# Top-4 routing in an adaLN transformer block: all experts for all tokens, or 128-row tiles of the tokens that chose an expert

## The chip, the cores and the metric

One core of a Trainium2 chip runs the whole program in one launch. The metric is the device time of that core in microseconds, the median over runs. The core has TensorE (PE, matmuls into PSUM), VectorE (DVE), ScalarE (ACT), GpSimd (POOL), SyncE (SP, which only issues DMAs here) and 16 DMA engines that all queues share.

## What is computed

Two batches of 512 tokens, 256 channels. Each half of the block normalises the rows, scales and shifts them by values made from a condition vector, and adds a gated branch. The first branch is a gated linear recurrence with an MLP behind it. The second, which the change is about, is a mixture of experts:

```python
h = layernorm(x) * (1 + cb) + sb                       # (2, 512, 256)
scores = softmax(h @ gate_weight.T)                    # 16 experts
topk_weight, topk_idx = top_k(scores, 4)
for e in range(16):                                    # hidden width 176 each
    w_e = sum(where(topk_idx == e, topk_weight, 0))
    y = y + w_e[:, None] * glu_ffn(h, gate_up[e], down[e])
y = y + glu_ffn(h, shared_gate_up, shared_down)        # hidden width 352
x = x + gb * y
# glu_ffn(x, gu, d): g, u = split(x @ gu.T); (silu(g) * u) @ d.T
```

So of 1024 x 16 (token, expert) pairs, 4096 have a weight other than zero.

## The kernel before

Each engine runs its own list of steps, written out by hand in `TENSOR_PLAN`, `SCALAR_PLAN`, `VECTOR_PLAN` and `POOL_PLAN` (lines 79 to 118); a step name is a function and its arguments (`up.0.3` is `ff_up(0, 3)`), and semaphores join the lists. In the plans, work of batch 1 is woven into that of batch 0, one stage apart. An engine executes in its list's order, so a wait holds everything behind it on that engine.

Products of full precision are made of three fp32r matmuls: each operand is split into a high part, rounded to fp32r, and a low rest, and high x high, low x high and high x low are summed in PSUM. ScalarE writes the high parts, VectorE (activations) and GpSimd (weights, `low`, line 372) the rests. Other matmuls are plain fp32. Activations stand with channels on the partitions, 512 tokens of one batch in the columns.

In the second half, the MLP of the first branch ends with `down.b.7`; `tm` turns its sum to token rows, VectorE adds and gates it (`sum3`, `gated3`, `plus_x`, lines 985 to 999), takes statistics (`var3`), GpSimd takes the power -0.5 (`rstd`, line 430), `hn3` normalises, `t3` transposes back to channels, ScalarE applies scale and shift (`h3`, line 484), `logits` multiplies by the gate weights, and `lgsub`, `exp`, `topk` make the weights of the four chosen experts, zero for the others. `weights_out` transposes them, SP writes them to DRAM and reads each expert's row back broadcast over partitions (`load_gate`, line 330).

The 16 x 176 routed and 352 shared hidden units are laid end to end and cut into 25 slices of 128, of which 22 (`NR`) are routed. For each slice SP loads 384 KB of weights (`wmoe`), ScalarE and GpSimd split them, and for each batch `moe_up` makes 12 matmuls of 512 columns (lines 1399 to 1401), ScalarE applies silu (line 700), VectorE multiplies by the gate (line 1056) and by the up half (line 1060), both split the product (lines 706 and 1065), and `moe_down` adds 6 matmuls (lines 1432 to 1436) into two banks that sum over all 25 slices. Batch 1 follows batch 0 eight slices behind (`LEAD`), so the first slices of batch 0 stand in the plans between the last steps of batch 1's own gate, and from then on TensorE alternates between the batches. At the end `sum_out` scales by `gb`, `sum_to_tokens` (line 1454) transposes, `finish` (line 1092) adds and SP stores 256 KB pieces of `hm`.

Early in the plans, SP brings six chunks of 512 KB of the MLP's weights through two `stage` buffers (line 319), each after the chunk two before was split by GpSimd (lines 372, 416).

Of the kernel before, what the change touches and what calls it, by code (L numbers as in the profile page):

```python
# [5 lines left out]
FP32R = mybir.dt.float32r  # L6
ALU = mybir.AluOpType
# [37 lines left out]
GATES = 3
ORDER = [NR, NR + 1, *range(6), NR + 2, *range(6, NR)]


def tile_of(q):

    return ORDER[q % NM]


def step_of(b, i):

    return i + LEAD * b


def gated_tile(b, i):

    return tile_of(step_of(b, i)) < NR


def gate_number(b, i):

    return sum(gated_tile(b, j) for j in range(i))


def gate_pieces(t):

    edges = sorted({t * P, (t + 1) * P, *(e * FE for e in range(NE + 1) if t * P < e * FE < (t + 1) * P)})
    return [(a // FE, a - t * P, b - t * P) for a, b in zip(edges, edges[1:])]

# [6 lines left out]
    down.0.4 t2.1 up.0.7 down.0.5 up.1.0 down.0.6 down.0.7 up.1.1 tm.0 up.1.2 down.1.0 up.1.3 down.1.1 down.1.2 up.1.4  # L83
    t3.0 up.1.5 down.1.3 up.1.6 logits.0 down.1.4 down.1.5 up.1.7 wt.0 down.1.6 down.1.7 eup.0.0 tm.1 eup.0.1 eup.0.2
    edown.0.0 edown.0.1 eup.0.3 edown.0.2 eup.0.4 t3.1 eup.0.5 edown.0.3 eup.0.6 logits.1 edown.0.4 eup.0.7 edown.0.5
    edown.0.6 wt.1
# [4 lines left out]
    wsm.3 wsm.4 q.0 xconv.0 sqk.0 sqv.0 ig.0 rk.0 rv.0 ga.0 wsm.5 h1hi.1.0 h1hi.1.1 h1.1.0 h1.1.1 sqm.0 og.0 rm.0 q.1  # L91
    sqo.0 k.1 wsm.6 ro.0 v.1 gated.0 xconv.1 wo.0 ig.1 ga.1 rk.1 h2hi.0.0 h2hi.0.1 h2.0.0 h2.0.1 rv.1 silu.0.0 og.1
    hid.0.0 silu.0.1 sqm.1 hid.0.1 silu.0.2 rm.1 silu.0.3 sqo.1 ro.1 gated.1 hid.0.2 silu.0.4 wo.1 hid.0.3 hid.0.4
    silu.0.5 silu.0.6 hid.0.5 hid.0.6 h2hi.1.0 h2hi.1.1 silu.0.7 h2.1.0 h2.1.1 silu.1.0 hid.0.7 hid.1.0 acc.0 silu.1.1
    silu.1.2 hid.1.1 ehigh.0.0 silu.1.3 hid.1.2 silu.1.4 hid.1.3 h3.0 silu.1.5 silu.1.6 hid.1.4 hid.1.5 exp.0 hid.1.6
    ehigh.0.1 silu.1.7 ehigh.0.2 hid.1.7 acc.1 ehigh.0.3 esilu.0.0 ehid.0.0 esilu.0.1 ehid.0.1 esilu.0.2 ehid.0.2
    ehigh.0.4 esilu.0.3 ehid.0.3 ehigh.0.5 esilu.0.4 ehigh.0.6 h3.1 esilu.0.5 esilu.0.6 ehid.0.4 ehigh.0.7 ehid.0.5
    exp.1 ehid.0.6 esilu.0.7 ehigh.0.8 ehid.0.7 ehigh.0.9
# [10 lines left out]
    hidlo.1.5 topk.0 hidlo.1.6 prod.1.7 wt.0 hidlo.1.7 egated.0.0 sum3.1 egated.0.1 gated3.1 elo.0.0 egated.0.2 elo.0.1  # L109
    plus_x.1 var3.1 elo.0.2 egated.0.3 hn3.1 elo.0.3 egated.0.4 egated.0.5 elo.0.4 egated.0.6 lgsub.1 h3lo.1 elo.0.5  # L110
    elo.0.6 topk.1 egated.0.7 wt.1 elo.0.7
# [5 lines left out]
    rstd.0.3 elow.1 elow.2 elow.3 elow.4 rstd.1.3 elow.5 elow.6 elow.7  # L117
# [10 lines left out]
def adaln_block_kernel(nc, x, cT, wmod, par, wsm, wff, wout, wgate, wmoe, sel, mats, out):  # L128
    ctx = ExitStack()
    with ctx:  # L130
# [36 lines left out]
        gm = [sb(f"gm{b}", [P, KC, T]) for b in range(NB)]  # L167
# [49 lines left out]
        def s(name):  # L217
            return S[name]
# [64 lines left out]
        def _(sp):  # L283
# [1248 lines left out]
```

## Time and profile before

| | us |
|---|---|
| median of 3 runs | 386.26 |
| lowest, highest | 385.79, 460.69 |
| profiled execution, span from the first to the last instruction | 383.2 |
| TensorE busy in it | 368.9 (96%) |
| VectorE, ScalarE, GpSimd busy | 245.5, 200.2, 111.0 |
| DMA, mean over the span | 91 GB/s |

The profile is of one execution. Its page gives the span alone and no time around it; the lowest run, 385.79, is 2.6 us above the span. Matmuls are pipelined, and a matmul's busy time in the groups holds its way through the array; how often one can start is read from the distance of two.

### The profile page before, as it was taken

Reading aid. Unit: us, or ns where it says so; the run is one execution under the profiler, and the core shown is the slowest. Engines: PE = TensorE matmul, PEld = TensorE weight load, DVE = VectorE, ACT = ScalarE, POOL = GpSimd, SP = SyncE. Lnnn points to the kernel's source line nnn. Section 1 sums busy time; section 2 is a strip of 40 time slices with the busy share of each in tenths; the row PEclk is TensorE's granted clock in tenths of the full one; section 3 lists DMA queues with packets and bytes.
Section 4 is the critical chain, followed back from the end, with each engine's and each line's share of the span. In section 5 each row is a group of like instructions: output and inputs, shape, how many; then the busy total and the mean of one; then the engine's idle time right before and its main releaser. Section 6 shows DMA issues by size and latency. Waiting matters only on the chain.

```text
span 383.2 us, 4573 instructions
## 1 busy us (share of the span) xinstructions
PE 368.9 (96%) x1590; PEld 286.2 (75%) x1590; DVE 245.5 (64%) x439; ACT 200.2 (52%) x314; POOL 111.0 (29%) x94
## 2 busy tenths in 40 slices
PE   6997988999999999999999999999999999999995
PEld 3774656656788888888878888888888888888883
DVE  4799985796765484749593555655555565555664
ACT  3679968788745326544654443333343333344441
POOL 1492769400010030315433123211112311133310
PEclk9899999999999999999999999999999999999998
DMA  6911131000030010162524622344333333125321
GB/s 222 362 31 42 50 109 62 2 0 0 9 131 2 0 41 3 44 164 71 137 85 152 193 97 96 97 126 134 126 98 96 96 102 129 45 70 149 125 85 55
DMA packets 18967, 34.81 MB, mean 91 GB/s; under 512 B 2528, under 2 KB 6496, under 8 KB 18944
## 3 DMA queue, kind: packets, MB, share of 16 engines
q1 hardware_dynamic: 18944, 34.52, 28.8%
q8 instruction: 13, 0.21, 0.2%
q14 instruction: 10, 0.08, 0.1%
HBM read 33.39 MB, written 1.11 MB: 90 GB/s over the span
## 4 chain that ended last, share of the span: by engine, by line
PE 83%; DVE 7%; ACT 4%; DMA 2%; SPq 2%; issue 1%; POOL 0%; DVEq 0%; ACTq 0%
PE ps L1399 12%; PE ps L1401 12%; PE ps L1400 12%; PE ps L1432 6%; PE ps L1436 6%; PE ps L1433 6%; PE ps L1351 4%; PE ps L1356 4%; PE ps L1352 4%; PE ps L1117 3%; PE ps L1134 3%; PE ps L1118 3%; DMA w<-in_wsm 2%; DVE w L857 1%; PE ps L1303 1%
## 5 line engine op out<-in xcount | busy, mean ns | idle before, releaser
L372 POOL TENSOR_TENSOR wsm_lo<-w,wsm_hi 128x768 fp32r<-128x768 f32 (+1 forms) x40 | 71.2, 1784 | 204.1 <-ACT wsm_hi L694 183.2
L1399 PE MATMUL ps<-b_hi,wsm_hi 128*128 128x512 f32 x200 | 79.3, 396 | 0.0
L1401 PE MATMUL ps<-b_lo,wsm_hi 128*128 128x512 f32 x200 | 78.9, 395 | 0.0
L1400 PE MATMUL ps<-b_hi,wsm_lo 128*128 128x512 f32 x200 | 78.9, 395 | 0.0
L706 ACT ACTIVATE a_hi<-w 128x512 fp32r<-128x512 f32 x50 | 31.6, 632 | 86.4 <-DVE w L1060 83.5
L1056 DVE TENSOR_TENSOR w<-w,gate_b 128x512 f32<-128x512 f32 x44 | 43.1, 980 | 41.6 <-ACT w L700 41.6
L1065 DVE TENSOR_TENSOR a_lo<-w,a_hi 128x512 fp32r<-128x512 f32 x50 | 34.6, 693 | 31.6 <-ACT a_hi L706 31.5
L700 ACT ACTIVATE w<-ps 128x512 f32<-128x512 f32 x50 | 29.9, 597 | 34.7 <-PE ps L1401 34.6
L1399 PEld LDWEIGHTS ps<-b_hi,wsm_hi 128*128 128x128 f32 x200 | 37.7, 188 | 8.9 <-POOL wsm_lo L372 0.2
L1401 PEld LDWEIGHTS ps<-b_lo,wsm_hi 128*128 128x128 f32 x200 | 37.7, 188 | 8.9
L1400 PEld LDWEIGHTS ps<-b_hi,wsm_lo 128*128 128x128 f32 x200 | 37.7, 188 | 8.5
L1060 DVE TENSOR_TENSOR w<-w,ps 128x512 f32<-128x512 f32 x50 | 34.4, 688 | 14.9 <-PE ps L1401 11.4
L1432 PE MATMUL ps<-a_hi,wsm_hi 128*128 128x512 f32 x96 | 38.0, 396 | 0.0
L1433 PE MATMUL ps<-a_hi,wsm_lo 128*128 128x512 f32 x96 | 37.8, 394 | 0.0
L1436 PE MATMUL ps<-a_lo,wsm_hi 128*128 128x512 f32 x96 | 30.1, 394 | 0.0
L694 ACT ACTIVATE wsm_hi<-w 128x768 fp32r<-128x768 f32 x33 | 27.5, 834 | 0.1
L1351 PE MATMUL ps<-b_hi,wff_hi 128*128 128x512 f32 x64 | 26.7, 418 | 0.0
L1352 PE MATMUL ps<-b_hi,wff_lo 128*128 128x512 f32 x64 | 25.2, 394 | 0.0
L464 ACT ACT_TABLE_LOAD x17 | 21.8, 1283 | 1.0 <-PEq L1526 0.7
L1432 PEld LDWEIGHTS ps<-a_hi,wsm_hi 128*128 128x128 f32 x96 | 18.1, 188 | 4.2
L1436 PEld LDWEIGHTS ps<-a_lo,wsm_hi 128*128 128x128 f32 x96 | 18.1, 188 | 4.2
L1433 PEld LDWEIGHTS ps<-a_hi,wsm_lo 128*128 128x128 f32 x96 | 18.1, 188 | 4.2
(189 smaller groups left out, 581.7 us busy)
## 6 DMA issues: line engine op xcount, KB each, us to landing
w<-in_wmoe SPq DMA_DIRECT2D x33, 384.0 KB, 3.2
gate_b<-w_rows SPq DMA_DIRECT2D x16, 256.0 KB, 4.2
stage<-in_wff SPq DMA_DIRECT2D x4, 512.0 KB, 6.5
gate_b<-w_rows SPq DMA_DIRECT2D x8, 224.0 KB, 3.4
w<-in_wsm SPq DMA_DIRECT2D x3, 512.0 KB, 9.1
w<-in_x SPq DMA_DIRECT2D x3, 512.0 KB, 3.6
gate_b<-w_rows SPq DMA_DIRECT2D x8, 192.0 KB, 3.5
gate_b<-w_rows SPq DMA_DIRECT2D x8, 160.0 KB, 3.3
```

Source lines behind the costliest of these rows:

```text
L372: return nc.gpsimd.tensor_tensor(lo, raw, f32(hi), ALU.subtract)
L1056: nc.vector.tensor_tensor(first[:, j, :], W[b][1][:, j, :], gate_b[b][:, n % GATES, :], ALU.mult).then_inc(s(f"mprod{b}"), 1)
L1060: nc.vector.tensor_tensor(W[b][3][:, j, :], first[:, j, :], up_bank, ALU.mult).then_inc(s(f"mgated{b}"), 1)
L1065: nc.vector.tensor_tensor(a_lo[b][:, j, :], W[b][3][:, j, :], f32(a_hi[b][:, j, :]), ALU.subtract).then_inc(s(f"mlo{b}"), 1)
L1351: mm(out, wff_hi[:, k, o:o + P], b_hi[b][:, k, :], start=k == 0, stop=False)
L1352: mm(out, wff_lo[:, k, o:o + P], b_hi[b][:, k, :], start=False, stop=False)
L1399: mm(bank, mgu(wsm_hi, slot, k, which), b_hi[b][:, k, :], start=k == 0, stop=False)
L1400: mm(bank, mgu(wsm_lo, slot, k, which), b_hi[b][:, k, :], start=False, stop=False)
L1401: last = mm(bank, mgu(wsm_hi, slot, k, which), b_lo[b][:, k, :], start=False, stop=k == KC - 1)
L1432: mm(PS[2 * b][:, m, :], mdn(wsm_hi, slot, m), a_hi[b][:, j, :], start=i == 0, stop=False)
L1433: mm(PS[2 * b][:, m, :], mdn(wsm_lo, slot, m), a_hi[b][:, j, :], start=False, stop=False)
L1436: last = mm(PS[2 * b][:, m, :], mdn(wsm_hi, slot, m), a_lo[b][:, j, :], start=False, stop=False)
```

## The change

Only the pairs that exist are computed, in plain fp32. Its parts:

- `rank.b` (TensorE and VectorE) gives each pair the slot `1 + 1024 e + (number of earlier tokens that chose e)` by matmuls of the chosen-matrix with a triangle of ones. GpSimd scatters each token's row of 288 floats (256 channels, 16 weights, its number, padding) to its four slots in a DRAM array `xs_rows`, by 16 indirect DMAs of 128 rows per batch. ScalarE's `fill` has written an empty row, with a weight of zero and a spare number, to every one of the 16,512 slots before, and zeros to four arrays `acc_rows`.
- `rows.b`: TensorE, ScalarE and GpSimd make the modulated rows with tokens on the partitions.
- `table` makes, on every partition, for each of 47 tiles its first slot, its expert's offset into the up weights and into the down weights. 47 is the most that 4096 pairs in 16 groups can fill; tiles past the last one read empty rows.
- Weights of all experts are loaded once, unsplit: `wdown` over buffers that the first half used, `wup` over the MLP's weights when the MLP is done.
- The three shared slices are computed as before, for all tokens, now in the plans, and summed to `hm`.
- A loop over 47 tiles follows on every engine, with four stages one step apart (`xt`, `up`, `hid`, `down`). SP reads the slot from SBUF into a register and loads 128 rows (ring of four). TensorE transposes them, reads the offset, makes 2 matmuls of 352 columns, transposes the hidden 128x176 in two, reads the other offset, makes 2 matmuls of 256 columns. ScalarE copies `xT`, applies silu, copies `y` scaled with the row's weight. VectorE makes number and weight from the row, multiplies silu and up, copies `hT`. GpSimd adds `y` to one of the four `acc_rows` by an indirect, accumulating DMA.
- Then SP loads the four sums (2 x 512 KB each), VectorE adds them, multiplies by `gb` and adds to `hm`, and SP stores.

The plans, cut to where they differ:

```diff
 TENSOR_PLAN
-    ... tm.0 up.1.2 ... up.1.7 wt.0 down.1.6 down.1.7 eup.0.0 tm.1 eup.0.1 eup.0.2
-    edown.0.0 edown.0.1 eup.0.3 edown.0.2 eup.0.4 t3.1 eup.0.5 edown.0.3 eup.0.6 logits.1 edown.0.4 eup.0.7 edown.0.5
-    edown.0.6 wt.1
+    ... tm.0 rows.0 up.1.2 ... up.1.7 rank.0 down.1.6 down.1.7 eup.0.0 tm.1 rows.1
+    eup.0.1 edown.0.0 eup.0.2 t3.1 edown.0.1 logits.1 edown.0.2 eup.1.0 rank.1 eup.1.1 st.0 edown.1.0 eup.1.2 edown.1.1
+    edown.1.2 st.1
 SCALAR_PLAN
-    wsm.3 wsm.4 q.0 xconv.0 ...
+    wsm.3 wsm.4 q.0 fill xconv.0 ...
 VECTOR_PLAN
+    hidlo.1.5 topk.0 hidlo.1.6 prod.1.7 rank.0 hidlo.1.7 egated.0.0 sum3.1 gated3.1 elo.0.0 plus_x.1 var3.1 egated.0.1
+    hn3.1 elo.0.1 egated.0.2 h3lo.1 lgsub.1 elo.0.2 topk.1 egated.1.0 rank.1 table sum.0 elo.1.0 egated.1.1 finish.0
+    elo.1.1 egated.1.2 elo.1.2 sum.1 finish.1
 POOL_PLAN
-    rstd.0.3 elow.1 elow.2 elow.3 elow.4 rstd.1.3 elow.5 elow.6 elow.7
+    rstd.0.3 rows.0 elow.1 scatter.0.0 elow.2 scatter.0.1 rstd.1.3 scatter.0.2 rows.1 scatter.0.3 scatter.1.0
+    scatter.1.1 scatter.1.2 scatter.1.3
```

The new functions, cut:

```diff
+RW = C + 2 * NE
+NTILE = (NB * T * TOPK + NE * (P - 1)) // P
+XROWS = 1 + DUMMY + P
+AROWS = CAP + P
 # SP
+            sp.wait_ge(s("down_done"), NB * NF)
+            for k in range(KC):
+                for which in range(2):
+                    o = (2 * k + which) * P
+                    sp.dma_start(wup[:, k, which, :].rearrange("p (t n) -> p t n", n=P),
+                                 wmoe[0:NR, :, o:o + P].rearrange("t p n -> p t n")).then_inc(s("wexp_in"), 16)
+            sp.wait_ge(s("scattered"), 16 * NB * NT * TOPK)
+            sp.wait_ge(s("tab_ready"), 1)
+            for i in range(NTILE):
+                if i >= RING:
+                    sp.wait_ge(s("xt_psum"), i - RING + 1)
+                    sp.wait_ge(s("wv_ready"), i - RING + 1)
+                row = nc.sync.value_load(tab[0:1, 0, i:i + 1], min_val=1, max_val=1 + DUMMY)
+                sp.dma_start(xt[:, i % RING, :], xs_rows[bass.ds(row, P), :]).then_inc(xt_in[i % RING], 16)
 # GpSimd
+            def scatter(b, j):
+                if j == 0:
+                    pool.wait_ge(s("filled"), 16 * (1 + NACC))
+                    ...
+                    pool.wait_ge(s("slots_ready"), b + 1)
+                for k in range(TOPK):
+                    nc.gpsimd.indirect_dma_start(
+                        xs_rows[:, :], bass.IndirectOffsetOnAxis(slots[b][:, j, k:k + 1], 0), h3x[b][:, j, :], None
+                    ).then_inc(s("scattered"), 16)
+            def add_rows(i):
+                n = i % NACC
+                pool.wait_ge(s("y_sb"), i + 1)
+                pool.wait_ge(s("wv_ready"), i + 1)
+                if i >= NACC:
+                    pool.wait_ge(added[n], 16 * (i // NACC))
+                nc.gpsimd.indirect_dma_start(acc_rows[n][:, :], bass.IndirectOffsetOnAxis(ids[:, i:i + 1], 0),
+                                             ysb[n], None, compute_op=ALU.add).then_inc(added[n], 16)
 # ScalarE
+            def fill():
+                act.wait_ge(s("fill_ready"), 1)
+                act.dma_start(xs_rows[1:XROWS, :].rearrange("(r p) c -> p r c", p=P),
+                              empty.unsqueeze(1).broadcast_to([P, XROWS // P, RW])).then_inc(s("filled"), 16)
+                for n in range(NACC):
+                    act.dma_start(acc_rows[n][:, :].rearrange("(r p) c -> p r c", p=P),
+                                  empty[:, 0:C].unsqueeze(1).broadcast_to([P, AROWS // P, C])).then_inc(s("filled"), 16)
 # TensorE
+            def tile_up(i):
+                ...
+                pe.wait_ge(s("xt_sb"), i + 1)
+                if i >= 2:
+                    pe.wait_ge(s("h_ready"), i - 1)
+                e = nc.tensor.value_load(tab[0:1, 1, i:i + 1], min_val=0, max_val=(NE - 1) * FE)
+                for k in range(KC):
+                    last = mm(bank(1, i)[:, 0:2 * FE].rearrange("p (w n) -> p w n", w=2), xT[i % 2][:, k * P:(k + 1) * P],
+                              up[:, k, :, bass.ds(e, FE)], start=k == 0, stop=k == KC - 1)
+                last.then_inc(s("up_psum"), 1)
+            def tile_down(i):
+                ...
+                e = nc.tensor.value_load(tab[0:1, 2, i:i + 1], min_val=0, max_val=(NE - 1) * 2 * C)
+                for h in range(2):
+                    last = mm(bank(3, i)[:, 0:C], hT[i % 2][:, h * P:(h + 1) * P], down[:, bass.ds(e + h * C, C)],
+                              start=h == 0, stop=h == 1)
+                last.then_inc(s("y_psum"), 1)
+            for step in range(NTILE + 3):
+                if step < NTILE:
+                    xt_in_channels(step)
+                if 0 <= step - 1 < NTILE:
+                    tile_up(step - 1)
+                if 0 <= step - 2 < NTILE:
+                    hid_in_channels(step - 2)
+                if 0 <= step - 3 < NTILE:
+                    tile_down(step - 3)
```

## Rows read from the trace of the kernel before

**Rows 1.** The page: busy share of TensorE and its granted clock in 40 slices, tenths.

```profile
PE   6997988999999999999999999999999999999995
...
PEclk9899999999999999999999999999999999999998
```

**Rows 2.** The page: the chain that ended last, shares of the span by engine, by line.

```profile
PE 83%; DVE 7%; ACT 4%; DMA 2%; SPq 2%; issue 1%; POOL 0%; DVEq 0%; ACTq 0%
PE ps L1399 12%; PE ps L1401 12%; PE ps L1400 12%; PE ps L1432 6%; PE ps L1436 6%; PE ps L1433 6%; PE ps L1351 4%; PE ps L1356 4%; PE ps L1352 4%; PE ps L1117 3%; PE ps L1134 3%; PE ps L1118 3%; DMA w<-in_wsm 2%; DVE w L857 1%; PE ps L1303 1%
```

**Rows 3.** Busy us of each engine in a stretch of the expert stage.

```profile
206.00:340.00 134.00, 134.00 (x579) 108.65 (x578) 74.02 (x96) 51.14 (x80) 29.87 (x17) 1.00 0.36 111
```

**Rows 4.** The chain in order of time: start us, us, what.

```profile
40.06 1.72 PE ps L1303 x4
...
162.56 0.47 PE ps L1134 x2
165.82 0.87 PE ps L1174 x8
...
190.14 1.69 PE ps L1385 x16
...
207.25 0.46 PE ps L1436 x2
...
332.73 0.46 PE ps L1436 x2
```

**Rows 5.** Groups by line and form: busy us, mean ns of one, idle before.

```profile
L1399 PE MATMUL ps<-b_hi,wsm_hi 128*128 128x512 f32 x200 | 79.3, 396 | 0.0
...
L372 POOL TENSOR_TENSOR wsm_lo<-w,wsm_hi 128x768 fp32r<-128x768 f32 x33 | 62.3, 1889 | 183.2 <-ACT wsm_hi L694 183.2
...
L372 POOL TENSOR_TENSOR wff_lo<-stage,wff_hi 128x1024 fp32r<-128x1024 f32 x4 | 9.5, 2394 | 0.0
...
L764 DVE TENSOR_SCALAR w<-hm,mv,rr 128x256 f32<-128x256 f32 x24 | 8.3, 410 | 2.8 <-POOL rr L430 2.8
...
L430 POOL TENSOR_TENSOR rr<-rr,const 128x4 f32<-128x4 f32 x6 | 6.5, 1084 | 0.5
...
L484 ACT ACTIVATE w<-ps,modc 128x512 f32<-128x512 f32 x4 | 3.1, 778 | 2.2 <-PE ps L1167 2.2
...
L1092 DVE TENSOR_TENSOR hm<-hm,ps 128x512 f32<-128x512 f32 x4 | 2.6, 682 | 0.7 <-PE ps L1454 0.7
...
L988 DVE TENSOR_TENSOR hm<-hm,ps 128x1024 f32<-128x1024 f32 x2 | 2.4, 1218 | 0.1
```

**Rows 6.** SP's issues (start us, us) and DMAs from issue to landing (KB each, us).

```profile
4.25 0.43 SPq L306 DMA_DIRECT2D par_sb<-in_par  x1
...
8.23 1.44 SPq L286 DMA_DIRECT2D w<-in_wsm  x1
...
w<-in_x SPq DMA_DIRECT2D x3, 512.0 KB, 3.6
...
out<-hm SPq DMA_DIRECT2D x4, 256.0 KB, 2.6
...
cT_sb<-in_cT SPq DMA_DIRECT2D x1, 2.0 KB, 1.6
```

**Rows 7.** Early windows: busy us of each engine, clock, DMA share, GB/s.

```profile
8.00:10.00 2.00, 0.60 (x3) 0.20 (x3) 1.87 (x5) 0.00 (x0) 0.00 (x0) 1.00 1.00 335
16.00:18.00 2.00, 2.00 (x7) 1.25 (x6) 1.55 (x7) 1.58 (x3) 2.00 (x3) 0.50 1.08 368
4.00:8.00 4.00, 3.66 (x10) 1.75 (x9) 2.47 (x10) 0.50 (x2) 0.00 (x0) 1.00 0.92 298
```

**Rows 8.** GpSimd in order of time: start us, us, operation, idle before and releaser.

```profile
51.41 1.04 POOL L416 CAST wout_hi<-stage 128x1024 fp32r<-128x1024 f32 x1 [1.06 <-DMA stage<-in_wout]
```

**Rows 9.** VectorE in order of time, the gate of batch 1.

```profile
191.87 0.43 DVE L1017 MAX8 top<-ps 128x8 f32<-128x16 f32 x4
...
197.29 1.39 DVE L1037 SCALAR_TENSOR_TENSOR wres<-rep,sc 128x64 f32<-128x64 f32 x1
```

More of the change, by code:

```diff
@@ L43 @@
 NR = NE * FE // P
+NS = NM - NR
+SHARED = [NB * NF + b * NS for b in range(NB)]
 ALL = 2
[L45 to L72, printed above, removed]
+CAP = NB * T
+NTILE = (NB * T * TOPK + NE * (P - 1)) // P
+HALF = FE // 2
+RW = C + 2 * NE
+ID = C + NE
+DUMMY = NE * CAP
+XROWS = 1 + DUMMY + P
+NACC = 4
+AROWS = CAP + P
+RING = 4
 TENSOR_PLAN = """
@@ L437, in _ @@
+            def add_rows(i):
[6 more added lines that the diff above has]
+                                             ysb[n], None, compute_op=ALU.add).then_inc(added[n], 16)
             steps = {
+                "rows": modulated_rows, "scatter": scatter,
@@ L444, in _ @@
                 steps[name](*args)
-            for q in range(LEAD, NQ):
-                moe_low(q)
+            for i in range(NTILE):
+                add_rows(i)
         @block.scalar
@@ new lines, in _, with rest @@
+            for step in range(NTILE + 2):
+                if step < NTILE:
+                    meta(step)
+                if 0 <= step - 1 < NTILE:
+                    tile_hid(step - 1)
+                if 0 <= step - 2 < NTILE:
+                    ht_out(step - 2)
+            def rest(b, k):
+                dve.wait_ge(acc_in[k], 16 * NB)
+                dve.wait_ge(s("rows_sb"), 2 * NB)
+                given = tok(W[b][k if k < 2 else 5 - k])
+                if k == 0:
+                    return
+                first = tok(W[b][0])
+                if k > 1:
+                    dve.wait_ge(s("dve_order"), at["sum", b])
+                at["sum", b] = done(nc.vector.tensor_tensor(first, first, given, ALU.add))
@@ L1468, in _ @@
-            for q in range(NM, NQ):
-                moe_up(1, q - LEAD)
-                moe_down(1, q - 1 - LEAD)
-                if q == NM + 1:
-                    sum_to_tokens(0)
-            moe_down(1, NM - 1)
-            sum_to_tokens(1)
+                last.then_inc(s("tw_psum"), 1)
+            steps = {
+                "warm": warm, "ones": ones, "scale": scale, "shift": shift, "t1": t1, "gate": gate, "chan": chan, "q": q, "qlo": qlo, "k": k, "klo": klo, "v": v,
+                "ig": ig, "iglo": iglo, "ga": ga, "ssk": ssk, "og": og, "ssv": ssv, "u": u, "mem": mem, "oc": oc, "vo": vo, "wo": wo, "tw": tw, "t2": t2,
+                "up": ff_up, "down": ff_down, "tm": tm, "t3": t3, "logits": logits, "rank": rank, "rows": rows, "st": sum_to_tokens,
+                "eup": moe_up, "edown": moe_down,
+            }
@@ new lines, in _, with xt_in_channels @@
+            for name, args in plan(TENSOR_PLAN):
+                steps[name](*args)
+            up = wup[:, :, :, :]
+            down = wdown[0:HALF, :, :].rearrange("p g c -> p (g c)")
+            def xt_in_channels(i):
+                if i == 0:
+                    pe.wait_ge(s("msum_sb"), 1)
+                    pe.wait_ge(s("msum_dve"), 1)
+                pe.wait_ge(xt_in[i % RING], 16 * (i // RING + 1))
+                if i >= 2:
+                    pe.wait_ge(s("xt_sb"), i - 1)
+                for c in range(KC):
+                    last = nc.tensor.transpose(bank(0, i)[:, c * P:(c + 1) * P], xt[:, i % RING, c * P:(c + 1) * P], ident)
+                last.then_inc(s("xt_psum"), 1)
```

522 lines of the change are left out of this document (331 added, 191 removed).

## The prediction, made before the changed kernel ran

> **What bounds the kernel now.** I read the slices first: TensorE is at 9 tenths from the eighth slice to the last but one, and its clock is full [rows 1]. The shares of the chain say the same: 83% of what ended last is TensorE, and the largest lines are the six of the expert stage [rows 2]. The windows then show how that stage differs from the rest: from 206 to 340 us TensorE is busy 134.00 of 134.00 us, VectorE 74, ScalarE 51, GpSimd 30, the DMA engines 0.36 [rows 3]. Nothing but TensorE limits it. In the chain in order of time the last matmuls of a down step come every 4.18 us: from 207.25 to 332.73 are 31 such pieces, 30 intervals, 125.48 / 30 = 4.18 us [rows 4]. One interval holds one 128-wide slice of the hidden units for one batch, 12 up and 6 down matmuls, so one 512-column fp32r matmul occupies the array for 4.18 / 18 = 0.232 us; the mean of 0.396 us in the groups holds the pipeline's depth [rows 5] and is not what a matmul costs.
>
> **What goes.** 22 routed slices x 2 batches x 4.18 us = 184 us of TensorE, all of it on the path, and with it the multiplication by the gate, the weight splits and the gate rows' DMAs, which lay beside it. The 3 shared slices per batch stay.
>
> **What comes, in the order of the path.**
>
> *Before the experts.* The expert stage starts at 162.6, beside the last piece of the MLP [rows 4]. Up to there three things are added. `fill` puts five DMA issues on ScalarE at about 22 us; an issue took 0.61 and 0.43 us on SP [rows 6], so some 2.5 us, on an engine that leads into the chain there. The fill writes 129 x 128 rows of 1152 bytes and 4 x 1152 rows of 1 KB, 19.0 + 4.7 = 23.7 MB. Loads ran at 298 GB/s with rows of 1 KB and 2 KB [rows 7]; at that rate it takes 80 us and ends near 105 us, 60 us before the first scatter wants it; this cover is gone only below 170 GB/s. Meanwhile it shares the DMA engines with the last four weight chunks, and GpSimd waited 1.06 us for one of these already [rows 8]: I take another 1.5 us for it. `rows` and `rank` for batch 0 are some 22 records of 128 columns or fewer on TensorE, 0.109 us each as in the transposes (8 in 0.87 us [rows 4]), less the four transposes removed: 2 us. Together 6 us: the expert stage starts at 168.6.
>
> GpSimd's new constants I cost at nothing: it writes them at the start, behind those that TensorE's first step waits for, and its first work for others needs weights that have to be loaded first.
>
> *The row chain of batch 1.* This was hidden behind 30 us of routed matmuls; now nothing follows TensorE's shared work but the tiles, and those need every token ranked. From 168.6: first up step 12 x 0.232 = 2.8, `tm` 0.9, to 172.3. Then on VectorE two 128x1024 additions and one multiplication, 1.22 each, statistics 4 x 0.41 and 0.6, two interleaved steps of 0.68, GpSimd's small pair 1.04 + 0.4, normalisation 4 x 0.41 [rows 5]: with handovers 11 us, 183.3. Transposes 0.9, ScalarE's four passes of 0.78, logits 1.7 [rows 4, 5]: 189. From the first MAX8 at 191.87 to the end of the weights at 198.68 it took batch 1 6.8 us [rows 9]; with less between, I take 6, to 195. `rank.1` 12 records of 0.109 and two handovers, then six small VectorE operations: 3 us, 198. TensorE's six shared slices (25 us) and the small steps end by about the same time.
>
> *The scatters.* 32 indirect DMAs on GpSimd, 16 of them after the last rank. No row shows one. From below: a plain issue on SP, 0.43 us [rows 6]; from above: GpSimd's own largest pass over 128x1024, 2.39 us [rows 5]. I take 1.2, nearest to GpSimd's small power step of 1.04 us, since a sequencer program computes 128 addresses. Batch 0's sixteen can start at 166. Eight of them and an `elow` of 1.89 stand in front of batch 1's power step: 177.5, and its variances come at 179, so they just fit; the other eight, with `rows.1` of 2 x 2.39 between, end at 195, before 198. Then 16 x 1.2 = 19, landing 2.6 as the output's did, and one tile load with a register read in front, 0.5 + 0.4 + 2.6 [rows 6]: the first tile is there at 224. TensorE has then waited some 25 us. At 0.43 us each it would be 211. At 2.4 us batch 1's power step waits until 187, batch 0's last scatter ends at 213, batch 1's at 251, and the first tile is there at 257. Behind SP's wait for all 32 stand the tile loads, and behind those the whole loop.
>
> The expert weights, 5.8 MB in rows of 512 bytes and 2.9 MB in rows of 1 KB, are 29 us of DMA at 298 GB/s from 168.6 on; wanted at 224. The short rows may halve the rate, which would use all of that cover and not more.
>
> *The 47 tiles.* A plain fp32 matmul of 512 columns is two records and 0.86 us (4 records in 1.72 [rows 4]), so 1.68 ns a column. Per tile: up 2 x 352 columns 1.18 us, down 2 x 256 columns 0.86, four transposes 0.44: 2.48 us of array, 117 us for 47. The software pipeline gives every handover a step of slack. ScalarE has three passes of at most 256 columns, half of what takes it 0.78 [rows 5], VectorE about five of 1.5 us together, SP one load, GpSimd one accumulating scatter at 1.2, four in flight: all under 2.48. What I doubt is TensorE's own sequencer: two reads of an expert's offset from SBUF into a register per tile, with bounds checks and addresses that are computed, behind which the matmuls stand. No row shows a register read. From below it is hidden, 0 us (it is added work, so no gain); from above one whole memory round trip each, as the smallest load has from issue to landing, 1.6 us [rows 6], 3.2 a tile. The reads stand behind 1.1 and 1.4 us of queued array work, so I expose 0.46 us each, near the SP issue row, 0.92 a tile: 3.40 us a tile, 47 x 3.40 = 160, and 4 us for the three steps that run out. The Trainium skill ("DMA: Bandwidth & Descriptors", Latency and other measured facts) gives a floor of about 600 ns for such a load; taken as fully exposed it would make an estimated 2.48 + 1.2 = 3.7 us a tile and 173 us in place of 160, which no trace here shows yet.
>
> *The end.* Last y copy 0.4, scatter 1.2, landing 2.6, two 512 KB loads 0.4 + 4.3 (one landed in 3.6), VectorE 2 x 1.22 additions, 2 x 1.22 multiplications, 4 x 0.68 additions = 7.6, output issue and landing 3 [rows 5, 6]: 20 us.
>
> Sum: 224 + 160 + 4 + 20 = 408 us of span. The profiled execution before has 383.2; the runs' median is 386.26, 3.1 above it, so 411 us, +6%.
>
> **The point of balance.** With 248 us outside the loop, a tile of (383.2 - 248) / 47 = 2.88 us gives no change. What this kernel's measurement can tell from no change is 2%: below 2.71 us a tile it is faster, above 3.04 slower.
>
> **The rivals.**
> A, array paced: register reads hide behind queued matmuls and a scatter costs 1.0 us. First tile at 221, 47 x 2.48 = 117, 4, 20: 362, so 365 us, faster. For it: no other engine is near 2.48 us, and matmul issue in the present stage keeps a record per 0.109 us [rows 4]. Against: 94 reads with nothing in the trace to show them cheap. 0.23.
> B, GpSimd's scatters are the price: 2.4 us each, first tile at 257, loop 160, 24: 441, so 444 us. For it: every GpSimd row is the slowest of its kind, 2.39 against VectorE's 1.22 for 1024 columns [rows 5]. 0.16.
> C, half clock in the loop: the array's 2.48 becomes 4.96, 47 x 4.96 = 233, 224 + 233 + 24 = 481, so 484 us. For it: the granted clock, still 1.00 from 8 to 10 us, where TensorE was busy only 0.60 of 2 us, was down at 0.50, the lower of its two levels (1.2 GHz), from 16 to 18 [rows 7]; in the loop a fifth of the array's work is transposes and a quarter of the time waiting, and in front of it lie 25 idle us. Against: from the third slice on the clock stands at 9 tenths or more, with TensorE at 7 and 8 tenths in some [rows 1]. 0.09. The Trainium skill ("TensorE: Matmul & The Clock Gate", Part 4) has it that transposes do not count as TensorE being busy, which speaks for C and against this change; the transposes of this trace stand eight at a time between matmuls and don't decide it.
> D, ScalarE or SP's loads stand still behind the fill: five issues that block for a good part of 80 us, 40 us of them on the chain: 408 + 40, so about 451 us. For it: SP's issues grew from 0.4 to 1.44 us with eight loads outstanding [rows 6]. Against: they never grew more. 0.06.
>
> **How the numbers follow.** My forecast 0.46, A 0.23, B 0.16, C 0.09, D 0.06. The forecast's own range, tiles of 2.9 to 4.0 us and scatters of 0.9 to 1.6, is 383 to 446. The range given, 362 to 465 us, takes in A and B and leaves out C and what lies past D. Faster by over 2%: A and a little of my own low side, 0.25; within 2% 0.14; slower 0.61.
>
> **What would show it.** Right: six shared slices done near 200 us, TensorE idle until about 224, tiles at 3.4 us with PE's waits put down to issue rather than to ACT, DVE or DMA, clock full, about 20 us behind the last down matmul. A shows as tiles of 2.5 us with PE near 9 tenths; B as GpSimd busy or its queue taken all through 166 to 251, and PE waiting for a DMA; C as a clock of 0.5 in the loop; D as ScalarE's queue standing at 22 us, and an expert stage that starts past 190. I am wrong in the mechanism if the tiles wait for `added` or `xt_in`, since I gave both four steps of slack.

## The result, and the profile after

Median 453.68 us (452.82 to 456.54, 4 runs) against 386.37 for the kernel before: ratio 1.175, 95% interval 1.170 to 1.180. Slower, as forecast, but by 17.5% where 6.4% was predicted: 453.7 lies in the range of 362 to 465, and 43 us above the number. The ratio leaves out one of the kernel before's four runs, of 460.69 us, in a slower state of the chip.

The page of the kernel after: slices (beside [rows 1]), shares of the chain (beside [rows 2]), four groups and two DMA issues.

```profile
PE   6940000089989999989997476719999999999500
ACT  2700000289779775532642341103444444444200
PEclk9995555589999999999999668858999999999955
DMA  7799999951210007711039911233676767775692
...
issue 30%; PE 25%; POOL 23%; DVE 7%; DMA 6%; ACT 4%; ACTq 3%; SPq 1%; POOLq 1%; DVEq 0%
...
L511 POOL DMA_INDIRECT acc_rows<-w,ids x47 | 73.4, 1561 | 57.6 <-ACT w L834 57.3
L1694 PE MATMUL ps<-wup,w 128*128 x188 | 65.6, 473 | 0.5 <-issue 0.5
L1329 PE MATMUL ps<-b_hi,wsm_hi 128*128 128x512 f32 x8 | 4.3, 533 | 63.1 <-ACT b_hi L645 63.1
L542 ACT ACT_TABLE_LOAD x17 | 21.8, 1283 | 65.6 <-issue 64.7
...
xs_rows<-xt ACTq DMA_DIRECT2D x1, 18576.0 KB, 60.8
acc_rows<-xt ACTq DMA_DIRECT2D x4, 1152.0 KB, 12.9
```

The first thing to see is the hole: from the fourth slice to the seventh every engine is at 0, and the DMA row is at 9. In the groups, TensorE and ScalarE have a wait of 63.1 and 64.7 us, which is one and the same: TensorE waits for ScalarE's `b_hi`, and ScalarE's own wait is put down to "issue", so to nothing but its own instruction stream. The 23% of GpSimd in the chain are no second bound: the chain is followed back from the last accumulating scatter, and in the loop 57.3 of GpSimd's 57.6 us of idle time before these scatters are waits for ScalarE's copy of `y`, so they keep the tiles' pace and do not set it. ScalarE in order of time names the instruction (beginning us, duration us, engine; ACTq is its queue of issues):

```profile
21.78 0.42 ACTq L771 DMA_DIRECT2D xs_rows<-xt  x1
21.98 0.58 ACT L603 ACTIVATE w<-ps 128x512 f32<-128x512 f32 x1
22.23 54.33 ACTq L774 DMA_DIRECT2D acc_rows<-xt  x1
22.45 0.59 ACT L603 ACTIVATE w<-ps 128x512 f32<-128x512 f32 x1
76.59 11.08 ACTq L774 DMA_DIRECT2D acc_rows<-xt  x3
87.70 1.28 ACT L542 ACT_TABLE_LOAD   x1 [64.67 <-issue]
```

The first of `fill`'s five issues took 0.42 us, although it moves 19.0 MB (the page's 18,576 KB; one expectation below writes 18.6 MB). The second, of 1.2 MB on the same queue, stood for 54.3 us, the next three for 11.1. ScalarE does nothing from 23.0 to 87.7 us. The windows show that all else stops with it (us, then busy us of each engine, granted clock, DMA share, GB/s), and what the tile loop looks like (beside [rows 3]):

```profile
30.00:60.00 30.00, 0.00 (x0) 0.00 (x0) 0.00 (x0) 0.00 (x0) 0.00 (x0) 0.53 1.03 335
60.00:90.00 30.00, 0.00 (x0) 0.00 (x0) 0.00 (x0) 2.25 (x3) 0.00 (x0) 0.50 1.02 329
...
320.00:420.00 100.00, 100.00 (x481) 73.96 (x480) 38.92 (x197) 42.49 (x120) 62.34 (x40) 1.00 0.69 107
```

In the loop TensorE is busy 100.00 of 100.00 us at full clock. TensorE in order of time (beside the pieces of [rows 4]):

```profile
323.15 0.38 PE L1707 MATMUL ps<-mats_sb,sg 128*88 128x128 f32 x2
323.37 1.03 PE L1720 MATMUL ps<-wdown,w 88*128 x4
324.23 0.38 PE L1681 MATMUL ps<-mats_sb,xt 128*128 128x128 f32 x2
324.45 1.35 PE L1694 MATMUL ps<-wup,w 128*128 x4
325.64 0.38 PE L1707 MATMUL ps<-mats_sb,sg 128*88 128x128 f32 x2
```

From one tile's transposes (L1707) at 323.15 to the next at 325.64 are 2.49 us, and no idle time stands in brackets.

The parts of the span side by side. The first tile starts on TensorE at 301.5 us (predicted 224), the last down matmul ends at 424.4, so the loop is 122.8 (164), and 26.9 remain (20): 77.5 late, 41.2 early, 6.9 late, together the 43.3 us between 451.3 and 408. So two large errors of opposite sign stand behind a miss of 43.

### The profile page after: what moved, and what is told of

It reads as the page before. It is cut to its first block, busy times and chain, and to the rows that moved or that the text cites. A ratio compares the mean times of both kernels' runs of the same rounds, so it can differ in the third digit from the quotient of the medians.

```text
span 451.3 us, 5495 instructions
## 1 busy us (share of the span) xinstructions
PE 321.8 (71%) x1410; PEld 236.2 (52%) x1410; DVE 209.2 (46%) x582; ACT 176.4 (39%) x341; POOL 173.9 (39%) x160
## 4 chain that ended last, share of the span: by engine, by line
issue 30%; PE 25%; POOL 23%; DVE 7%; DMA 6%; ACT 4%; ACTq 3%; SPq 1%; POOLq 1%; DVEq 0%
POOL acc_rows L511 16%; POOL xs_rows L500 5%; PE ps L1528 3%; PE ps L1533 3%; PE ps L1529 3%; PE ps L1294 3%; ACTq L774 3%; PE ps L1311 3%; PE ps L1295 2%; DMA acc_rows<-w,ids 2%; DMA w<-acc_rows 2%; DMA w<-in_wmod 1%; POOL wsm_lo L405 1%; DVE b_lo L884 1%; PE ps L1329 1%
## 5 line engine op out<-in xcount | busy, mean ns | idle before, releaser
L511 POOL DMA_INDIRECT acc_rows<-w,ids x47 | 73.4, 1561 | 57.6 <-ACT w L834 57.3
L1694 PE MATMUL ps<-wup,w 128*128 x188 | 65.6, 473 | 0.5 <-issue 0.5
L1329 PE MATMUL ps<-b_hi,wsm_hi 128*128 128x512 f32 x8 | 4.3, 533 | 63.1 <-ACT b_hi L645 63.1
L1720 PE MATMUL ps<-wdown,w 88*128 x188 | 48.6, 381 | 0.7 <-DVE w L1247 0.6
L542 ACT ACT_TABLE_LOAD x17 | 21.8, 1283 | 65.6 <-issue 64.7
L500 POOL DMA_INDIRECT xs_rows<-h3x,slots x32 | 33.8, 1055 | 26.6 <-issue 20.0
L1694 PEld LDWEIGHTS ps<-wup,w 128*128 128x128 f32 x188 | 33.1, 196 | 11.5 <-issue 1.9
L834 ACT ACTIVATE w<-ps,wv 128x256 f32<-128x256 f32 x47 | 22.2, 473 | 37.0 <-PE ps L1720 37.0
L1329 PEld LDWEIGHTS ps<-b_hi,wsm_hi 128*128 128x128 f32 x8 | 2.0, 254 | 64.6 <-issue 63.9
L1720 PEld LDWEIGHTS ps<-wdown,w 88*128 88x128 f32 x188 | 31.9, 190 | 4.1 <-issue 1.6
L1528 PE MATMUL ps<-b_hi,wff_hi 128*128 128x512 f32 x64 | 26.9, 421 | 2.0 <-ACT w L728 1.5
L1533 PE MATMUL ps<-b_lo,wff_hi 128*128 128x512 f32 x64 | 20.2, 396 | 0.0
```

Of the source, the lines that this page charges most:

```text
L500: nc.gpsimd.indirect_dma_start(xs_rows[:, :], bass.IndirectOffsetOnAxis(slots[b][:, j, k:k + 1], 0), h3x[b][:, j, :], None).then_inc(s("sc ...
L511: nc.gpsimd.indirect_dma_start(acc_rows[n][:, :], bass.IndirectOffsetOnAxis(ids[:, i:i + 1], 0), ysb[n], None, compute_op=ALU.add).then_in ...
L542: nc.scalar.preload_act_table_set(name)
L834: nc.scalar.activation(ysb[i % NACC], bank(3, i)[:, 0:C], ACT.Copy, scale=wv[:, i:i + 1]).then_inc(s("y_sb"), 1)
L1528: mm(out, wff_hi[:, k, o:o + P], b_hi[b][:, k, :], start=k == 0, stop=False)
L1533: last = mm(out, wff_hi[:, k, o:o + P], b_lo[b][:, k, :], start=False, stop=k == KC - 1)
```

## The experiments

**Who holds ScalarE?** Theory: an issue that comes behind a large DMA on the same queue stands until most of that DMA has been taken; then the order and the queue of the five decide, not their bytes. Rival: 23.7 MB keep the DMA engines busy, and all who need them wait, in whatever order. First the order:

```diff
-                act.dma_start(xs_rows ...)      # 19.0 MB
                 for n in range(NACC):
                     act.dma_start(acc_rows[n] ...)
+                act.dma_start(xs_rows ...)
```

> The changed kernel with the five fill DMAs on ScalarE's queue in the other order: the four of 1.2 MB first, the one of 19.0 MB last; same bytes, same queue, same place. Theory Q (an issue behind a big DMA on the same queue stands until nearly all of that DMA's descriptors are taken, and the 54 us are ScalarE standing there): the four small ones cost about 0.4, 3, 3, 3 us, the big one goes behind them after 3 to 4 us, ScalarE stands for 11 to 14 us in place of 65, and the time falls by about 50 us, from 454 to 400 to 408. Theory B (the DMA engines are full of the fill, and the loads that the chain needs are late, whoever issues what): nothing changes but a few us, 445 to 455.

405.41 us, ratio 1.047 [1.040, 1.054]. ScalarE in order of time:

```profile
22.15 0.39 ACTq L772 DMA_DIRECT2D acc_rows<-xt  x1
22.18 0.59 ACT L603 ACTIVATE w<-ps 128x512 f32<-128x512 f32 x1
22.57 6.36 ACTq L772 DMA_DIRECT2D acc_rows<-xt  x3
28.96 5.01 ACTq L774 DMA_DIRECT2D xs_rows<-xt  x1
34.01 1.28 ACT L542 ACT_TABLE_LOAD   x1 [11.23 <-issue]
```

The same five DMAs with the same bytes cost ScalarE 11.2 us in place of 64.7, and the time falls by 48 us. Then all but the large one were taken off ScalarE; SP issues the zeros later:

```diff
                 act.dma_start(xs_rows ...)
-                for n in range(NACC):
-                    act.dma_start(acc_rows[n] ...)
...
+            sp.wait_ge(s("fill_ready"), 1)
+            for n in range(NACC):
+                sp.dma_start(acc_rows[n] ...)   # behind the loads of x
```

> The changed kernel with the 19.0 MB DMA alone on ScalarE's queue at the same place, and the four zero fills of acc_rows issued by SP later, behind the second reload of x, when SP has nothing to do. Theory Q: ScalarE loses 0.4 us, so all 65 us go, less what the fill takes from the weight chunks and from x on the DMA engines, 0 to 6 us: 388 to 396 us. So the rest of the change would be worth about nothing against the kernel before (386.4). Theory B: 440 or more.

395.72 us, ratio 1.024 [1.017, 1.030], so 58 us less than the change itself. ScalarE goes on at once:

```profile
22.16 0.41 ACTq L775 DMA_DIRECT2D xs_rows<-xt  x1
22.18 0.59 ACT L607 ACTIVATE w<-ps 128x512 f32<-128x512 f32 x1
22.79 1.28 ACT L546 ACT_TABLE_LOAD   x1
```

That the queue counts, and not full DMA engines alone, one row of the kernel after shows already: SP issued a weight chunk on its own queue while the 19.0 MB were under way, in 0.54 us.

```profile
27.55 0.54 SPq L339 DMA_DIRECT2D wdown<-in_wff  x1
```

Last, what of the large DMA has to be gone before the next issue is let through. The same bytes in pieces of 4608 in place of 1152 (a few arrays grow; the second issue is now a small one of 144 KB, the last 128 rows of `xs_rows`):

```diff
-                              empty.unsqueeze(1).broadcast_to([P, XROWS // P, RW]))
+                              xt[:, :, :] as [P, 4 * RW], broadcast over DUMMY // P // 4)
```

> The changed kernel, fill in its place and order, but each partition writes four neighbouring rows of xs_rows in one piece of 4608 bytes: a quarter of the descriptors, the same 19.0 MB (acc_rows' spare rows are 512 in place of 128, 6.3 MB in place of 4.7). If the stand is set by the number of descriptors, the second issue takes about 54 / 4 = 14 us; if by the bytes that have to move, the big DMA takes 18.9 MB / 0.36 = 52 us or somewhat less and the second issue 40 to 50 us, since few of its pieces can be outstanding. I expect the bytes: 440 to 455 us in all.

446.28 us in its one run, 7 us under the change itself.

```profile
22.11 0.42 ACTq L771 DMA_DIRECT2D xs_rows<-xt  x1
22.12 0.59 ACT L603 ACTIVATE w<-ps 128x512 f32<-128x512 f32 x1
22.56 34.86 ACTq L774 DMA_DIRECT2D xs_rows<-xt  x1
57.46 22.27 ACTq L776 DMA_DIRECT2D acc_rows<-xt  x4
```

34.9 us, under the 40 to 50 expected if the bytes set it, and far over the 14 if the number of pieces did. The large DMA landed after 49.5 us, and the windows give 393 GB/s in this stretch, 326 in the kernel after. So the issue was let through 14 us ahead of the landing here, 6 us ahead there: an estimate of 5.6 MB in pieces of 4608 bytes, some 1,200, and of 2.0 MB in pieces of 1152, some 1,700. In pieces the two agree better than in bytes. That an issue waits until few enough pieces are left ahead of it on its queue fits both; how many, and whether the waiting issue's own pieces count (128 here, 1,152 there), two runs do not settle. An issue's own size did not hold it: the large one, of 16,512 pieces, took 0.42 us with none of `fill`'s issues ahead of it. The Trainium skill ("DMA: Bandwidth & Descriptors", Issuing engines are not separate DMA queues) says that issuing from several engines saves only the sequencer's time for the issue, "which is usually small relative to the DMA itself". The row of 54.33 us, of an issue of 1.2 MB, is an exception to this.

**What sets the tile?** Two register reads of an expert's offset per tile were the prediction's doubt. Both runs here stand on the kernel with the zeros from SP. In one they are doubled (each diff shows one of the two places):

```diff
                 e = nc.tensor.value_load(tab[0:1, 1, i:i + 1], ...)
+                e = nc.tensor.value_load(tab[0:1, 1, i:i + 1], ...)
```

> As e2_zeros_from_sp, but each of TensorE's two register reads of a tile is made twice, 94 reads more. The changed kernel's trace has 0.30 + 0.15 + 0.02 = 0.47 us for one and a tile every 2.49 us, which is the array's own 2.48. If the reads are wholly hidden behind queued matmuls with room to spare, the tile stays at 2.5 us and the time is that of e2. If they are just hidden, up to 0.94 us a tile shows, 47 x 0.94 = 44 us more. I expect 2.5 to 2.7 us a tile, 0 to 10 us more.

In the other TensorE reads none, so most tiles multiply by another expert's weights:

```diff
-                e = nc.tensor.value_load(tab[0:1, 1, i:i + 1], ...)
+                e = i // 6 * FE
```

> Built on the kernel with the zeros sent from SyncE (395.7 us, 2.49 us a tile, with two register reads of 0.47 us on TensorE's queue in each). Here TensorE reads no register: the expert of tile i is a constant, i // 6, so the tiles multiply by the wrong expert's weights for most rows; the sizes and the count of products are the same. The prediction's step (0.92 us of reads exposed in each tile, over a shorter array time) wants some 1.57 us a tile at best and 352 us in all; the theory that the array sets the pace and the reads lie wholly under its products wants 2.49 us a tile still and 394 to 397 us. Doubling the reads had cost 1.3 us a tile; if reads are half hidden, something between.

Doubled: 457.41 us, 62 more, or 1.3 us a tile, against 0 to 10 expected: a miss. None: 393.03 us, ratio 1.015 [1.010, 1.020], 2.7 us less than its base, whose interval it overlaps. The prediction's 0.92 us a tile would have been 43 us. TensorE in order of time, first doubled, where the gaps before a product are 0.54 and 0.72 us and from product to product pass 3.66 and 3.89 us; then without reads, where it is 2.49:

```profile
320.22 1.45 PE L1696 MATMUL ps<-wup,w 128*128 x4 [0.54 <-issue]
...
323.88 1.45 PE L1696 MATMUL ps<-wup,w 128*128 x4 [0.54 <-issue]
...
327.77 1.45 PE L1696 MATMUL ps<-wup,w 128*128 x4 [0.72 <-issue]
```

```profile
321.79 1.35 PE L1695 MATMUL ps<-wup,w 128*128 128x352 f32 x4
...
324.28 1.35 PE L1695 MATMUL ps<-wup,w 128*128 128x352 f32 x4
```

Taking the reads away leaves the pace at 2.49 us, so they are hidden and the array sets the pace. Adding as many again costs 1.3 us a tile where they last 0.94, so little is left of the cover, and the sequencer is the next bound; that rests on one run. A part of the excess has a row: in that run the first read before the up products lasts 452 ns in the median, in place of 303. The rest is open. What one read is, the line shows in the kernel after (min, median and max in ns):

```profile
L1692 PEldq TENSOR_LOAD <-tab x47: 295/302/482, 302.7 to 417.6; - x47
L1692 PEldq FUSED_REGOPS  x47: 151/151/165, 303.3 to 417.9; - x47
L1692 PEldq SEQ_ASSERT  x47: 18/18/24, 303.5 to 418.1; - x47
```

0.47 us in all, close to the 0.46 us of the prediction.

**Where do the other us before the first tile go?** In the kernel with the zeros from SP, where ScalarE is free, the first tile starts at 243.0 us, still 19 after the forecast. GpSimd has there one place that stands out, a scatter that starts 7.18 us late, in front of batch 1's power step, whose variances were ready 5.5 us before:

```profile
182.26 1.70 POOL L504 DMA_INDIRECT xs_rows<-h3x,slots  x1 [0.31 <-issue]
191.13 0.97 POOL L504 DMA_INDIRECT xs_rows<-h3x,slots  x1 [7.18 <-issue]
192.14 0.25 POOL L479 TENSOR_SCALAR rr<-mv 128x4 f32<-128x4 f32 x1
```

It lies beside `wup`'s load of 5.8 MB, and stands of about 2.1 us come again: of the 32 scatters the 8th, 15th, 22nd and 29th stand, so one after every seven. Two theories, two runs: the load is in the way, or the room for GpSimd's descriptors is full.

```diff
+            sp.wait_ge(s("hn2_ready"), 2 * NB)
             sp.wait_ge(s("down_done"), NB * NF)
             ...                                  # load wup
```

> Built on the same kernel: SyncE issues the four megabyte-sized loads of the up weights only once batch 1's normalised rows are ready (about 193 us), instead of at 173.6 us, where a scatter on GpSimd stood for 7.2 us and batch 1's inverse deviation, next but two in GpSimd's order, came at 192.5 us for variances ready at 186.7 us. If the stall is the scatter's descriptors waiting behind those loads on the DMA engines: the deviation at about 187 us, batch 1's chain and the first tile 4 to 6 us earlier, 389 to 392 us, the loads still done before the first tile. Rival: the stall comes from the scatters' own number (room for descriptors), moves by nothing, and the time is 395 to 397 us.

```diff
-    nc = bacc.Bacc(..., dynamic_dma_scratch_size=1024)
+    nc = bacc.Bacc(..., dynamic_dma_scratch_size=2048)
-RING = 4
+RING = 3
```

> Built on the same kernel: the room for GpSimd's DMA descriptors is 2048 in place of 1024 bytes a partition, and the ring of tile buffers is three in place of four to make room in SBUF. In the kernel it is built on, GpSimd stands 2.1 us after every eleventh or so of the 32 row scatters, and once 7.2 us beside the weights' load. If these stalls are waits for free descriptors, there are half as many: the scatters of batch 1 take 22 us instead of 24.3, batch 0's stall of 7.2 us shrinks or goes, and the time is 388 to 393 us. If they have another cause, the stalls stay as they are and the time is 395 to 397 us. A ring of three has 7.5 us for a load of 2.2 us and should cost nothing.

The later load: 394.03 us, ratio 1.017 [1.011, 1.023], not told apart from its base. The first stand is 3.90 us in place of 7.18, and the power step's first half comes at 189.6 in place of 192.1 us, but the next stand, now beside the moved load, grew to 6.02 us, and the total of stands was 22.9 us (21.0 before). More room: 388.17 us, ratio 1.002 [0.999, 1.006], 7.5 us under its base and clear of it. The group of the 32 scatters, at the old and at the doubled room (the second profile is of that kernel's slowest run, 391.65 us):

```profile
L504 POOL DMA_INDIRECT xs_rows<-h3x,slots x32 | 33.5, 1046 | 27.4 <-issue 21.0
```

```profile
L504 POOL DMA_INDIRECT xs_rows<-h3x,slots x32 | 33.8, 1057 | 20.3 <-issue 12.5
```

0.30 us between two scatters is their normal distance, 9.0 us over 30; of the 12.0 above it 3.5 are left. The places say it more sharply: with twice the room only the 15th and the 29th scatter stand, so the distance went from seven to fourteen. Room is what the scatters wait for. The ring of three buffers changed in the same run; the tiles keep their pace, and no run has it alone. A load beside the scatters makes such a wait long, in both runs that have one there (7.18 and 6.02 us); that the descriptors ahead are then taken late is the likely reason and not shown.

Then the row chain of batch 1 in the kernel with more room. VectorE computed two low halves beside GpSimd's `rows.1` in 4.51 us, ahead of the router's MAX8, and TensorE a shared tile ahead of the ranks. Neither is needed for the slots:

```diff
-    hn3.1 elo.0.1 egated.0.2 h3lo.1 lgsub.1 elo.0.2 topk.1 egated.1.0 rank.1 table
+    hn3.1 elo.0.1 egated.0.2 lgsub.1 topk.1 elo.0.2 h3lo.1 rank.1 egated.1.0 table
-    edown.0.2 eup.1.0 rank.1 eup.1.1
+    edown.0.2 rank.1 eup.1.0 eup.1.1
```

> Built on the kernel with more room for descriptors (388.2 us). There batch 1's router logits are complete on TensorE at about 198 us, but VectorE first computes the low halves of the normalised rows (4.5 us for two, beside GpSimd's modulated rows) and TensorE first runs one shared tile, so the slots come at 211.4 us. Here VectorE takes the top four before these low halves and TensorE counts the ranks before the shared tile: the slots should come at about 205 to 206 us. GpSimd ends batch 0's scatters at 208.2 us, so the first scatter of batch 1 would start at 208.5 in place of 212.2 us, and everything behind is 3 to 4 us earlier: 384 to 385.5 us. Rival: the shared tiles, delayed by this, end after the scatters have landed and hold the first tile up; then 387 to 390 us.

386.12 us, ratio 0.998 [0.995, 1.001]. Behind the router, with GpSimd's `rows.1` over, the two low halves take 1.28 us in place of 4.51. Batch 1's first scatter starts 1.04 us behind batch 0's last instead of 3.98; the gain over its base, 2 us, is under the forecast, and the two intervals overlap.

**The clock of the first tiles.** In the kernel with more room, too, TensorE stood idle for 8.8 us ahead of the loop. The first tile's up products then took 2.71 us, the second's 2.26, the later ones 1.35. Five products with no reader were put in front:

```diff
+            for i in range(5):
+                mm(bank(0, 0), gtmp[:, 0, 0:P], gtmp as [P, 512], start=True, stop=True)
             pe.wait_ge(s("tab_ready"), 1)
```

> Built on the same kernel: five plain products of 512 columns are put on TensorE before the tile loop, with no use of their result. TensorE stands idle for 8.8 us there, the granted clock is 0.64 in 230 to 240 and 0.67 in 240 to 250 us, and a product of the first tiles takes twice as long as later (2.71 against 1.35 us for four). If the clock of the first tiles follows from this idle time, they run at full clock, and the first accumulating scatter comes 2 to 3 us earlier: 385 to 387 us. Rival: the clock stays low or the added products themselves run slowly and delay the first tile: 388 to 391 us.

387.30 us, ratio 1.003 [0.999, 1.006]: not told apart from its base. The five were done 4.45 us before the first tile, too early: its products took 2.71 us again. In the combined kernel below they ended where the first tile began, its products took 1.45 us, and the clock stayed at 1.00 (windows from 230 us, first this kernel, then the combined one):

```profile
230.00:240.00 10.00, 4.69 (x11) 2.14 (x10) 0.81 (x6) 0.77 (x2) 0.96 (x1) 0.78 0.35 99
240.00:250.00 10.00, 9.87 (x41) 6.65 (x40) 3.60 (x19) 3.53 (x10) 2.12 (x2) 0.88 0.28 59
```

```profile
230.00:240.00 10.00, 8.01 (x31) 4.30 (x29) 3.51 (x9) 1.98 (x4) 1.93 (x2) 1.00 0.29 89
240.00:250.00 10.00, 9.24 (x41) 6.46 (x42) 3.60 (x19) 3.44 (x10) 1.64 (x2) 1.00 0.35 78
```

How much of that the five products did is not shown: in the combined kernel the shared work itself ended nearer to the first tile, which would have left 4.3 us idle, and no run has it without the five.

**The end.** One accumulator fewer, on the kernel with the zeros from SP:

```diff
-NACC = 4
+NACC = 3
```

> Built on the same kernel: three accumulators in place of four. Two loads of 0.5 MB fewer at the end (10.5 us for eight, so 2.6 us less), two VectorE sums of 1.18 us fewer, and 1.15 MB less to zero early; an accumulating scatter must land within three tiles, 7.5 us, against 1.55 us of issue and 3.7 to 3.9 us of landing. If the end is bound by loads and sums: 390 to 393 us, the tile pace unchanged at 2.49 us. Rival: the landing, or the order on one accumulator, becomes the wait, the tiles grow beyond 2.6 us and the time is over 398 us.

392.59 us, ratio 1.015 [1.009, 1.020], 3 us under its base as the first theory has it, though the intervals overlap. The six loads were issued over 8.40 us in place of 10.52, one pair of sums of 2.36 us is gone, and the tiles keep their pace. But from the start of the last accumulating scatter to the end pass 23.3 us in place of 25.0, so the tail itself shows 1.7 us.

**Together.** Room for descriptors, the earlier slots, the five products and three accumulators in one kernel:

> The two edits just named and three accumulators in place of four, on the kernel with more room for descriptors. If the gains are in series (3.7, 2.5 and 3 us): 378 to 381 us, faster than the kernel before by 1.5 to 2 per cent. If only the largest counts, because each waits for the same thing: 383 to 386 us, no difference from before.

383.67 us (10 runs), ratio 0.992 [0.989, 0.995]: in the range of the second forecast, 4.5 us under the kernel with more room, and told apart from the kernel before by 0.8%. Alone the earlier slots, the products and the third accumulator had given 2.1, 0.9 and 3.1 us, the last on another base; whether they add up in full these intervals do not settle. In its profile one thing was left that all these kernels have: GpSimd's power step for batch 0's second half of the block comes at 79.3 us, against 71.0 in the kernel before, and the theory is that the fill of 19.0 MB shares the DMA engines with the last weight chunks. So the fill went behind those:

```diff
-    wsm.3 wsm.4 q.0 fill xconv.0
+    wsm.3 wsm.4 q.0 xconv.0
-    ro.0 v.1 gated.0 xconv.1 wo.0
+    ro.0 v.1 gated.0 fill xconv.1 wo.0
```

> Built on the kernel with all edits together (383.7 us); only the place of the 18.6 MB fill in ScalarE's order is changed: behind batch 0's gated step, at about 66 to 70 us, when the last of the feed-forward weights have landed, instead of at 22 us. In that kernel the fill keeps the DMA engines full from 22 to 87 us; GpSimd waits 3.15, 0.63 and 0.94 us for weight chunks, and batch 0's second inverse deviation starts at 79.3 us, where it did at 71.0 us in the kernel before (29.3 against 27.5 us ahead of it). If the fill's contention with the weights' loads makes this difference: 6 to 8 us earlier there and 376 to 378 us in all, 2.3 to 2.7 per cent faster than the kernel before. Rival: the two are linked otherwise (the copies and waits that the change added there), the deviation stays near 79 us, and the time 382 to 385 us; or the fill now delays the loads behind it (the shared experts' weights at 113 to 124 us) and the gain is given back.

379.88 us (6 runs), ratio 0.984 [0.981, 0.988], a little short of the 376 to 378 expected. The waits for chunks and the power step in the combined kernel, and with the fill moved:

```profile
54.62 1.05 POOL L466 CAST wff_hi<-wdown 128x1024 fp32r<-128x1024 f32 x1 [3.15 <-DMA wdown<-in_wff]
...
79.25 0.23 POOL L479 TENSOR_SCALAR rr<-mv 128x4 f32<-128x4 f32 x1 [4.40 <-DVE mv L866]
```

```profile
52.15 1.03 POOL L466 CAST wff_hi<-wdown 128x1024 fp32r<-128x1024 f32 x1
...
73.81 0.23 POOL L479 TENSOR_SCALAR rr<-mv 128x4 f32<-128x4 f32 x1 [0.82 <-DVE mv L866]
```

The chunk's wait is gone and the power step 5.4 us earlier, as the theory has it. The fill now lies beside other loads: SP's three zero fills take 13.4 us to issue in place of 6.0, and two loads of weights behind them 9.1 in place of 4.2, but no engine's wait is put down to these loads. This version of the change beats both kernels: the kernel before by 1.6%, small but clear of the noise, the change as it was made by 16%.

## Why the prediction was wrong

The direction held, the size did not. By its own steps:

- *"`fill` puts five DMA issues on ScalarE ... so some 2.5 us".* This is the step that failed. The rows behind it were issues of small loads; what an issue costs behind 19.0 MB on its own queue was taken from them. It cost 65.5 us of ScalarE, 58 us of time. It was rival D, mechanism and place, though written with 40 us and given 0.06; the sign that spoke for it, SP's issues growing from 0.43 to 1.44 us behind eight loads [rows 6], was weighed too lightly. That D's 451 meets the 453.7 is luck: its 40 us were 18 short, and it kept the tile term, which was 41 us too long.
- *"Another 1.5 us" for the fill's contention.* Mis-sized: 5.4 us at the power step, 3.8 us of time.
- *"So I expose 0.46 us each": the tile of 3.40 us.* The second step that failed. The 2.48 us of array are right to 0.01; each read lasts 0.47 us, but none of it shows. Rival A was right on this term. The doubt of TensorE's sequencer had a ground: the doubled reads show it not far behind the array.
- *The chain of batch 1 and the scatters at 1.2 us.* The scatter is 0.96 us, 1.27 from start to start: right. Missing are the stands for descriptors (20.0 less 9.0 us in the kernel after; one of 6.20 holds up the power step for which scatters "just fit"), and VectorE's low halves, 4.5 us beside GpSimd in the kernel with more room, for which the sum has no term. Rival B (2.4 us a scatter) is refuted.
- *Half clock in the loop (C).* Refuted: 1.00 from 320 to 420 us, with four transposes in every tile. By the Trainium skill ("TensorE: Matmul & The Clock Gate", Part 4) a transpose does not count as TensorE being busy; in this loop, where up and down products lie between the transposes, that did not bring the clock down. Only the first tile's up products ran at half of it (2.71 us against 1.35), and part of the second's (2.18).
- *The end, 20 us.* 26.9: the output's tail was right, but the last scatter landed after 7.45 us, not 2.6, with the first of the eight loads issued beside it, and VectorE began its sums 13.6 us after its last tile.
- *GpSimd's constants, the expert weights' loads.* The tiles do not wait for either, as taken; but `wup`'s load lies beside the scatter that stood longest.
- *Smaller readings.* From span to run the sum adds 3.1 us; the profiled run of the kernel after has 1.8 (453.05 less 451.3). The issue of 0.61 us is not in [rows 6], and the clock's last slice in [rows 1] is at 8 tenths, not 9. None of these moves the outcome.

The mis-sized terms add up as in the parts above: +77.5 (58.5 of them go with ScalarE's stand, 19.0 are the rest), -41.2, +6.9. And without the stand of ScalarE, at 395.7 us, the change would have been 2.4% slower [1.7, 3.0]. Its profile says why (span 392.5 us, before 383.2): 184 us of routed matmuls are gone, and in their place come 123 us of loop, an end that is 21 us longer and, by what is left of the sum, 49 us before the first tile, 11 of them TensorE's last wait for the scattered rows.

## What to carry to other kernels

Before a DMA is put on the queue of an engine that computes, ask what is issued on that queue behind it: the first issue took 0.4 us here for 19.0 MB as for 1.2 MB, and the next stood for nearly all of the first one's transfer, and in the profile this is an "issue" wait on an engine whose neighbours all wait for it. Put a large transfer last on its queue and where no small load is awaited; with no work removed, the order alone was worth 48 us here, the other queue 58, and the later place 4 more. When a rival's mechanism is seen in a row, even small, price it with the sizes that the change brings and not with those of the row.

## What was not expected of the hardware

- An issue of 1.2 MB stood 54.3 us behind an issue of 19.0 MB that had itself taken 0.42 us; with pieces four times as long an issue of 144 KB stood 34.9 us.
- A register read from SBUF lasts 0.30 us and 0.17 us of register work. The Trainium skill's floor of about 600 ns ("DMA: Bandwidth & Descriptors", Latency and other measured facts) is above both together.
- Doubling these reads cost 1.3 us a tile where they last 0.94: some 0.15 us is one read that lasts longer, the rest is open.
- Indirect scatters of 128 rows of 1152 bytes are issued 1.27 us apart, the accumulating ones take 1.55 us each; the plain ones stood 2.1 us after every seventh, 7.2 beside a load, and after every fourteenth with double the room for descriptors.
- Pieces of 4608 bytes were written at 393 GB/s, pieces of 1152 at 326 to 335.
